# Attention in a two-layer block: contexts one quad at a time, score tiles in four PSUM banks, row maxima in three one-bank pieces

## What is computed

```
q, k, v = x @ Wq, x @ Wk, x @ Wv            # 16 heads of 8 columns, 2048 tokens
s = q @ k.T * scale ; s = where(causal, s, -inf)
out = softmax(s) @ v ; out = out @ Wo
```

## Time and profile before

| | us |
|---|---|
| median of three runs | 2043.42 |
| the profiled execution, its own time | 2041.5 |
| its span, first to last instruction | 2039.8 |
| TensorE busy | 1564.7 (77%) |
| VectorE busy | 1237.7 (61%) |
| ScalarE busy | 875.0 (43%) |
| GpSimd busy | 411.2 (20%) |

### The profile page before, as it was taken

How to read it: one execution, slowest core, us unless ns; L and a number is a source line. 1 busy time by engine, 2 the same in 40 slices (tenths; PEclk the granted TensorE clock), 3 DMA queues, 4 the chain that set the end, 5 groups by cost and what they waited for, 6 DMA issues and landing times.

```text
span 2039.8 us, 27036 instructions
## 1 busy us (share of the span) xinstructions
PE 1564.7 (77%) x8103; PEld 671.6 (33%) x8104; DVE 1237.7 (61%) x2336; ACT 875.0 (43%) x1663; POOL 411.2 (20%) x267
## 2 busy tenths in 40 slices
PE   4817756636999999999524912799999999868999
PEld 2302222321333333332213802233333333235665
DVE  2479999476777777774240115777777777324444
ACT  2353323010766667666301301166666666631111
POOL 4019989110000011010123061001001110000000
PEclk9958889965999999998757956599999999968999
DMA  2002213013111111110141122211111110000000
GB/s 69 6 29 81 82 62 114 0 51 91 36 37 48 34 37 47 36 35 13 52 132 49 50 49 93 49 37 36 48 36 35 47 45 26 13 16 8 23 15 29
DMA packets 59071, 91.76 MB, mean 45 GB/s; under 512 B 13001, under 2 KB 39057, under 8 KB 58993
## 3 DMA queue, kind: packets, MB, share of 16 engines
q1 hardware_dynamic: 56962, 86.79, 14.7%
q0 software_dynamic: 2048, 4.20, 0.9%
HBM read 74.63 MB, written 16.32 MB: 45 GB/s over the span
## 4 chain that ended last, share of the span: by engine, by line
PE 59%; DVE 23%; issue 6%; ACT 5%; POOL 3%; DMA 2%; DVEq 1%; SPq 1%; POOLq 0%; ACTq 0%
PE psum_a L870 16%; PE psum_b L840 11%; PE psum_a L852 9%; DVE arena L516 5%; DVE extra L1038 5%; DVE arena L490 3%; PE psum_a L1509 3%; PE psum_b L1509 3%; PE psum_b L326 2%; DVE extra L1041 2%; PE psum_a L326 2%; PE psum_b L1518 2%; ACT psum_a L432 2%; PE psum_a L1518 1%; POOL expert_inputs L1259 1%
## 5 line engine op out<-in xcount | busy, mean ns | idle before, releaser
L980 ACT ACTIVATE arena<-psum_a 128x512 f32<-128x512 f32 (+3 forms) x1280 | 585.6, 546 | 254.5 <-PE psum_a L852 152.5
L1038 DVE CUSTOM_DVE_ANT_0 extra<-psum_b,mask_q 128x128 bf16<-128x128 f32 (+7 forms) x512 | 365.4, 755 | 200.5 <-PE psum_b L840 200.2
L840 PE MATMUL psum_b<-arena 72*128 72x512 bf16 (+3 forms) x1280 | 362.3, 372 | 94.1 <-DMA arena<-k_parts 50.8
L852 PE MATMUL psum_a<-arena 75*128 75x512 bf16 (+3 forms) x1280 | 395.2, 357 | 11.4 <-ACT arena L980 4.5
L1041 DVE TENSOR_REDUCE extra<-psum_b 128x1 f32<-128x1024 f32 x256 | 300.6, 1219 | 64.0 <-PE psum_b L840 62.6
L870 PE MATMUL psum_a<-arena,extra 128*32 128x512 f32 x2560 | 336.6, 637 | 2.2 <-ACT arena L980 2.2
L852 PEld LDWEIGHTS psum_a<-arena 75*128 75x128 bf16 x1280 | 118.3, 98 | 337.9 <-ACT arena L980 156.7
L295 POOL TENSOR_TENSOR arena<-arena,extra 128x1024 f32<-128x1024 f32 x48 | 170.9, 3574 | 130.0 <-DVE arena L516 118.0
L840 PEld LDWEIGHTS psum_b<-arena 72*128 72x128 bf16 x1280 | 102.0, 100 | 241.4 <-DVE extra L1038 108.1
L786 POOL TENSOR_TENSOR arena<-arena 128x512 f32<-128x512 f32 x64 | 81.1, 1268 | 465.1 <-ACT arena L971 310.5
L971 ACT ACTIVATE arena<-psum_a 128x512 f32<-128x512 f32 x128 | 76.4, 597 | 137.5 <-PE psum_a L870 137.5
(11 more groups left out here) (263 smaller groups left out, 1707.8 us busy)
## 6 DMA issues: line engine op xcount, KB each, us to landing
arena<-q_parts SPq DMA_DIRECT2D x192, 96.0 KB
arena<-k_parts SPq DMA_DIRECT2D x192, 96.0 KB
extra<-c_rows SPq DMA_DIRECT2D x32, 512.0 KB, 3.6
arena<-in_L_ffn_fc_w_dram SPq DMA_DIRECT2D x32, 256.0 KB, 5.9
k_parts<-arena SPq DMA_DIRECT2D x10, 512.0 KB, 5.6
q_parts<-arena SPq DMA_DIRECT2D x6, 512.0 KB, 5.0
arena<-in_L_ffn_w_dram SPq DMA_DIRECT2D x24, 128.0 KB, 2.1
expert_inputs<-zeros SPq DMA_DIRECT2D x4, 512.0 KB, 6.0
```

Source lines behind the costliest of these rows:

```text
L840: m = e.matmul(ps[:, at:at + width], s.mq[0:ROWS, b, i * P:(i + 1) * P], s.mk[0:ROWS, b, c * CW:c * CW + width], start=True, stop=True)
L852: m = e.matmul(score_bank(p)[:, at:at + width], s.ek[0:ROWS + 3, b, j * P:(j + 1) * P], s.eq[0:ROWS + 3, b, (c + 1) * CW - width:(c + 1) * ...
L980: m = e.activation(probabilities(s, b, kind, quad, k, width), score_bank(p)[:, at:at + width], ACT.Exp)
L1038: m = e.tensor_tensor_reduce(s.unread[:, n % NB, at:at + length], ps[:, at:at + length], mask_q[:, 2 * CW - length:], 1.0, NEG, ALU.add, A ...
```

## The change

There are four score banks instead of three (`LOOK` = 4, all of `psum_a`). `psum_b` has three places of one bank for the ring (`NB` = 3), and the context bank is its fourth. A context set is one quad: ten sets per head instead of six. The maximum pass has 34 pieces of at most 512 columns: 10 of masked blocks (6 of them two row blocks that together fill 512 columns, 4 one block of 512) and 24 of one unmasked product of 512 columns. VectorE therefore has 16 masked and 24 unmasked reductions of a head, 40 in all, over the same 17408 columns. `mpart`, the table of partial maxima, has four columns per row block instead of two. `AHEAD_MAX` is 17.

```diff
-        LOOK = 3
+        LOOK = 4
...
-        SETS = [(0, [("diagonal", 0)]), (1, [("diagonal", 1), ("full", 0)]), (2, [("diagonal", 2), ("full", 1)]), (2, [("full", 2)]),
-                (3, [("diagonal", 3), ("full", 3)]), (3, [("full", 4), ("full", 5)])]
+        SETS = []
+        for c in range(NC):
+            SETS += [(c, [("diagonal", c)])] + [(c, [("full", c * (c - 1) // 2 + f)]) for f in range(c)]
...
-        MAX_PIECES = [([(0, 0, P, 0), (2, 0, 3 * P, P), (3, 0, CW, CW)], [(0, 0, 0, P, True), (2, 0, P, 3 * P, True), (3, 0, CW, CW, True)]),
-                      ([(1, 0, 2 * P, 0), (9, 2, 2 * P, 2 * P), (11, 2, CW, CW)],
-                       [(1, 0, 0, 2 * P, True), (9, 1, 2 * P, 2 * P, True), (11, 1, CW, CW, True)]),
-                      ([(8, 2, P, 0), (10, 2, 3 * P, P)], [(8, 1, 0, P, True), (10, 1, P, 3 * P, True)])]
-        MAX_PIECES += [([(i, 0, CW, 0), (i, 1, tail(i), CW)], [(i, 0, 0, CW + tail(i), True)]) for i in range(4, 8)]
-        MAX_PIECES += [([(i, 0, CW, 0), (i, 1, CW, CW)], [(i, 0, 0, 2 * CW, False)]) for i in range(8, 16)]
-        MAX_PIECES += [([(i, 2, CW, 0), (i, 3, tail(i), CW)], [(i, 1, 0, CW + tail(i), True)]) for i in range(12, 16)]
-        NB = 2
+        def max_piece(*reads):
+            at, products, taken = 0, [], []
+            for i, c in reads:
+                width = CW if c < i // 4 else tail(i)
+                products.append((i, c, width, at))
+                taken.append((i, c, at, width, c == i // 4))
+                at += width
+            return products, taken
+        MAX_PIECES = [max_piece((1, 0), (5, 1)), max_piece((9, 2), (13, 3))]
+        for g in range(NC):
+            MAX_PIECES += [max_piece((4 * g, g), (4 * g + 2, g)), max_piece((4 * g + 3, g))]
+            MAX_PIECES += [max_piece((i, c)) for i in range(4 * g, 4 * g + 4) for c in range(g)]
+        NB = 3
...
-        AHEAD_MAX = 9
+        AHEAD_MAX = 17
...
-            s.unread = extra[:, 1024:2048].bitcast(BF16).rearrange("p (b n) -> p b n", b=NB)
-            s.mpart = extra[:, 2048:2080].rearrange("p (t c) -> p t c", c=2)
+            s.unread = extra[:, 1024:2048].bitcast(BF16).rearrange("p (b n) -> p b n", b=4)
+            s.mpart = extra[:, 2048:2112].rearrange("p (t c) -> p t c", c=NC)
...
-            return psum_b[:, (n % NB) * 2 * CW:(n % NB + 1) * 2 * CW]
-        context_bank = psum_a[:, 3 * CW:4 * CW]
+            return psum_b[:, n % NB * CW:(n % NB + 1) * CW]
+        context_bank = psum_b[:, 3 * CW:4 * CW]
```

## The result

The changed kernel takes 1966.16 us (median of 4 runs, 1960.81 to 1966.64) against 2043.12 (4 runs): a ratio of 0.9617, 95% interval 0.9600 to 0.9634, or 77 us less. The profiled execution took 1966.64 us, its span 1964.9. Forecast were 1985 us and a range of 1952 to 2040.

A forecast was written before the change was run, and what follows sets the result against it. TensorE's work was taken to bound the heads, with ring waits in each pair, and VectorE the openings. 14 x -3.4 for pairs, +5 openings, -16 last pairs give -58.6: 1985 us, range 1952 to 2040.

The forecast's parts named there:

- floor with six sets: TensorE's own work in a pair of heads before the change, summed from start-to-start distances: 53.3 us.
- more context switches: On TensorE's path, ten single sets a head cost +2.1 us a pair, 0.26 per change to a context and back.
- clock: TensorE's clock in the loop: half its loss comes back as ring waits go, -0.6 us a pair, bounds +1.8 and -1.3.
- What is left, 5.9 us a pair, is waiting for the ring: Kernel before: 60.5 us a pair less 53.3 of TensorE's work and 1.3 of clock is TensorE waiting for VectorE's reads.
- The -4.9: Ring waits in the loop: 1.0 of 5.9 us stays, so -4.9 us a pair, bounds 0 and -5.9.
- The fourth score bank: Score tiles and ScalarE's exponentials in the loop: a later chunk copy is covered, cost 0; uncovered, 0.5 us at four places a head.
- the walk through t = 13 to 20: Worst place for the new ring, in the first head: TensorE arrives at 4.9, M0 is read at 5.3; 0.4 us a pair.
- the slower rival: Loop: ring waits stay and the switches add, 2078 us, chance 0.13; slower once more than about 3.7 us of wait remain.
- The opening: Opening stage of each attention, bounded by VectorE: +1.4, +0.8 and +0.7, less 0.4 for gaps; +2.5 us each, bounds +1 and +5.
- The last pair: End of each attention: first head -4.5, last head -3.5 us; -8 each, bounds 0 and -12.
- The bank-cycling rule: Skill page's warning of short idles between bank groups; rival: two more clock falls a pair, 2044 us, chance 0.06.
- the one in which nothing moves: Rival: ScalarE or the copies set the pace, so the whole stays about 2043 us, chance 0.02.

The follow-up runs named there:

- short reads, six sets: Changed kernel with six sets of before and each maximum over its first quarter of columns (times only): 1902.78 us, a pair 53.34.
- short reads, ten against six sets: Changed kernel, each maximum over its first quarter of columns: ten sets 1924.66 us, a pair 55.28; six sets 1902.78 us, a pair 53.34.
- short reads, kernel before: Kernel before with each maximum over its first quarter of columns, TensorE's and ScalarE's work unchanged (times only): 1948.95 us, a pair 55.47.
- fewer pieces ahead: Changed kernel with AHEAD_MAX 14 or 12 instead of 17: 1962.96 and 1960.83 us, a pair 56.96 and 56.67.

## Why the prediction was right, and where not

**The direction and the size of a pair were right, their account in part.** Forecast was -3.4 us a pair, measured -3.3 (60.5 to 57.18) over the five pairs of the prediction, and -3.8 as the mean of all twelve (60.8 to 57.05). That -3.3 came out so near is in part luck: the ring gave less than forecast and the clock more. The terms, with what they measured:

| term, us a pair | forecast | measured | by |
|---|---|---|---|
| floor with six sets | 53.3 | 53.34 | short reads, six sets |
| more context switches | +2.1 | +1.94 | short reads, ten against six sets |
| VectorE's work after | 47.5 | 47.2 | window |
| waits above the floor before, clock loss in | 7.2, of it 5.9 the ring's | 7.2: clock 1.0, VectorE 4.0, not VectorE's 2.1 | pairs at a clock of 1.00; short reads, kernel before |
| waits left after | 1.0 | 1.9 | 57.18 - 55.28 |
| clock | -0.6 | -1.0, all of it; -1.4 over all twelve pairs | 60.5 and 60.8 against 59.49 |

*"What is left, 5.9 us a pair, is waiting for the ring"* was the first step that failed. At a clock of 1.00 the kernel before has 59.49 - 53.34 = 6.15 us of waits, and 2.1 of them stay with VectorE short, now as waits for ScalarE's exponentials. The -4.9 measured 6.15 - 1.9 = -4.2. The fourth score bank, costed at 0 in the loop, is indeed at 0 beside single sets (57.18 and 57.11), and worth 0.5 beside double ones. The ring waits left were 1.9 instead of 1.0; the walk through t = 13 to 20 found 0.4 in one place, and what was left for the others was too little. Two slips in the working changed little: 136 products at 0.215 are 29.2, not 29.4, and in the slower rival the change turns slower at 5.9 - 2.1 - 5/14 = 3.4 us of wait, not 3.7.

**The switch was priced rightly and its gain was not seen.** The prediction charged single sets 2.1 us and credited the new ring with -4.9. The runs with full reads say otherwise:

| a pair, us | six sets | ten sets |
|---|---|---|
| two places of two banks, three score banks | 60.5 (59.49 at a clock of 1.00) | 56.99 |
| three places of one bank, three score banks | 58.03 | 57.11 |
| three places of one bank, four score banks | 57.54 | 57.18 |
| four places of one bank, three score banks | not run | 55.36 |
| two places of one bank, four score banks | not run | 65.08 |
| TensorE's floor | 53.34 | 55.28 |

Take each from its own floor. With six sets 7.2 us of waits and clock loss stand above it with the old ring, 4.7 with the new one, and 4.2 with the fourth score bank as well. With ten sets it is 1.7, 1.8 and 1.9. So it is the single sets that remove most of the waits, and they do it without the new ring; the ring alone removes 2.5 us, of it 1.0 clock. Why the single sets do it is argued, not shown. A double set keeps TensorE from refilling for 1.96 us; three places of 512 columns hold 1.8 us of reading, but two full ones of 1024 hold 2.3, so the lengths alone don't settle it. ScalarE has its share: the waits for exponentials that short reads laid bare stand behind double sets, and with single ones the chain of the old ring has none. With ten sets the new ring is no better than the old one in the loop (57.11 against 56.99). Its merit is that it needs three banks instead of four. The freed bank went to the scores, where it gains 2.2 to 3.7 us in a last pair and nothing in the loop; as a fourth ring place it gains 1.8 us in every pair.

**The opening** was forecast at +2.5 us, since VectorE bounds it. From the store of the key parts to the first score tile it went from 44.9 to 43.6: -1.3, and as much in the second attention. From VectorE's first read to the end of its last read of the opening:

```profile
471.28:505.48 34.20, 25.95 (x66) 5.02 (x64) 31.65 (x72) 0.70 (x2) 0.00 (x0) 0.50 0.24 53
470.94:504.31 33.37, 30.68 (x68) 6.51 (x66) 32.89 (x97) 0.56 (x2) 0.00 (x0) 0.50 0.27 61
```

VectorE's work grew by 1.2 us, where 2.9 were taken. Its idle time there fell from 2.6 to 0.5, where 0.4 less was allowed: before it waited for TensorE, at half clock, to fill 1024 columns. And its first read comes 0.6 us sooner behind the store (12.2 and 11.6 us), mostly since the first piece has two products instead of three. Both terms were mis-sized, and by enough to change the sign. Part of the first is that a reduction of 1024 columns took 1.18 us there, eight of them 9.49, and 1.13 in the loop; the rest was not followed up.

**The last pair** gained 13.5 and 9.1 us instead of 8. From its first sum to its last the clock rose from 0.88 to 1.00 in the first attention, and 0.12 of 55.1 us is 6.6; in the second it was 0.97 before and 0.95 after, and the 9.1 came without it. So the waits were sized too low: of the forecast 8, 4.5 stood for the first head, whose clock alone had been put at 5. The last head, from the end of the last set before it, took 25.4 us before and takes 19.3 now (932.39 to 951.68), where 21 was expected and TensorE's own work had been put at 19.2; -6.1 instead of -3.5. The fourth score bank is 2.2 to 3.7 of the gain. The last set, 3.26 us at half clock before, takes 1.07, and the waits of three exponentials are gone, as expected:

```profile
931.33 1.06 PE L876 MATMUL psum_b<-arena,extra 128*32 128x512 f32 x8
...
950.61 1.07 PE L876 MATMUL psum_b<-arena,extra 128*32 128x512 f32 x8 [0.51 <-ACT arena L986]
```
```profile
934.27 0.75 PE psum_a L858 x3
935.03 0.04 issue
935.07 1.07 PE psum_b L876 x8
```

**The whole by parts.** In both attentions together the openings gave -2.6 us where +5 was forecast, the pairs ahead of the last -49.8 where -47.6, and the last pairs -22.6 where -16. So of the 18 us beyond the forecast some 14 lie outside the loop, on which the argument rested.

**The bank-cycling rule.** The granted clock is 1.00 in all twelve loop windows with more, smaller pieces cycling through three banks, and in the three read of the kernel with two places, where TensorE waits most. By the Trainium skill (TensorE: Matmul & The Clock Gate, A second HAM failure mode: psum-queue depth-cycling) such short idles can make it fall again and again. In the windows of the loop no kernel with one-bank places shows that, and there the measurement decides; the kernel before, with two places of two banks, does lose its clock in most pairs of the loop, so the rule may bear on it. That rival, and the one in which nothing moves, are out. The slower one did not happen at three places and did at two.

Left open: which of score banks and piece shapes makes the 2.1 us; why single sets remove most of the waits; why the first pair of the first attention gained nothing; why fewer pieces ahead shorten a pair; and four places beside six sets, with a floor of 53.34, which was not run.

## What to carry to other kernels

Between a producer and a consumer in lock step, look at the longest single piece of other work in the producer's queue, and hold it against what the buffer keeps the consumer busy with; shortening that piece can be worth more than it costs in switches. To split a sum of waits, run the same kernel with the suspected consumer made short: it gives the share of that consumer, and its chain shows who holds the producer next. Before a freed buffer is given away, try it at each of its possible users; here the second user, a fourth ring place, was worth 21 us more than the first.

## What was not expected of the hardware

In the kernel with two places TensorE is busy less than in the kernel before and yet keeps its clock. A window of its loop, columns as in the earlier trace rows:

```profile
627.00:684.00 57.00, 52.94 (x324) 16.87 (x325) 41.52 (x109) 35.55 (x76) 4.37 (x5) 1.00 0.17 43
```

52.9 of 57 us busy at a clock of 1.00, against 58.06 of 61 at 0.97. Nor is a short idle stretch alone what brings the fall, as the prediction took from the earlier trace rows. The kernel before has another such stretch some 30 us later, and the kernel with two places a longer one, and behind neither does the clock fall:

```profile
646.00:648.00 2.00, 1.25 (x8) 0.62 (x8) 1.49 (x8) 1.66 (x5) 0.00 (x0) 1.00 0.00 0
648.00:650.00 2.00, 1.90 (x14) 0.50 (x16) 2.00 (x7) 1.50 (x3) 0.00 (x0) 1.00 0.06 12
```
```profile
659.00:661.00 2.00, 1.08 (x11) 0.35 (x12) 1.60 (x10) 1.32 (x4) 0.00 (x0) 1.00 0.00 0
661.00:663.00 2.00, 2.00 (x14) 0.55 (x14) 1.05 (x5) 0.86 (x2) 0.00 (x0) 1.00 0.05 10
```

What decides was not tried.
